# First attention of a four-layer kernel: one projection of queries and keys per batch, spread to head rows through DRAM

## The chip, the cores and the metric

The kernel runs on one NeuronCore of a Trainium2 chip. The metric is device time in microseconds (us) of the whole kernel, lower is better. The engines named are PE (TensorE, matmuls), DVE (VectorE), ACT (ScalarE), POOL (GpSimd) and SP (SyncE, which issues most of the DMAs). Each has its own queue of instructions, run in order, and they wait for each other by semaphores.

## The reference

Four layers, each an attention and a feed-forward part, over x of 4 batches x 512 tokens x 128 channels. The change touches the first attention only. It has H = 16 heads of 8 channels, a causal mask, and mixes the scores with a 3 x 3 kernel per head before the softmax:

```python
q = (x @ Wq).reshape(B, T, H, hd).transpose(0, 2, 1, 3)   # x normalised; k and v alike
attn = jnp.einsum('bhqd,bhkd->bhqk', q, k) * scale
kernels = softmax(kp.reshape(B, H, 9), axis=-1)           # kp from the context, per batch and head
attn0 = jnp.where(mask, 0.0, attn).reshape(1, B * H, T, T)
attn = conv(attn0, kernels 3x3, padding 1, one group per batch and head)
attn = jnp.where(mask, -jnp.inf, attn)
p = jax.nn.softmax(attn, axis=-1)
out = jnp.einsum('bhqk,bhkd->bhqd', p, v) ... @ proj_W + proj_b
```

## The kernel before, in words

A prologue (to about 82 us) loads weights, computes the 3 x 3 kernels from the context and builds constants. Then comes the first attention, `first_causal` (84 to about 465 us), with the start of the routing of the first feed-forward part. The rest isn't touched.

**The 3 x 3 mix as a matmul.** The score of a query row t and key column s after the mix is a sum over dy of queries shifted by dy and, over dx, of keys shifted by dx. So for each head 24 rows of the contraction are laid out: 3 shifts dy times 8 channels. `queries(G)` makes them for a group G of four heads (32 rows each, 128 in all) by three matmuls 128x512 against the weight tile `wq_rows`, which holds Wq's columns spread to these rows, each against a differently shifted x (`xnp`) and all added in one PSUM bank (bank 7). `keys(G)` is one matmul with `wk_rows`, which repeats a head's 8 columns three times. ACT copies the queries to `q3` (fp32) and, rounded, to `q3r`, and the keys to `kpad`. DVE mixes the keys over dx (`mixed_keys`: three instructions with a weight per row, `wcol`) into `kc`, ACT rounds that to `kcr`. Row 24 of each head carries the negated row maximum against a one in the keys.

**A group.** There are 16 groups G (four per batch b = G // 4). For each:
- far scores: 12 steps `max_scores` (L1379, fp32r matmuls of 32 rows into banks 0 and 1 in turn). DVE takes the maximum of each (`maxima`, L1694). Step n may start when the maximum of step n - 2 is taken.
- `maximum_out` puts the maxima in a tile, PE transposes it into bank 7 (`maximum_rows`, L1387), DVE adds it to `q3` (`maximum_in`, L1713).
- scores in three rounds (`scores`, L1400; the first needs `maximum_in`), exponentials on ACT (L1567), triangle select on POOL (L1296), product with v (`weighted`, L1411), copy, transposes, `outputs`.

**Near scores.** The entries next to the diagonal are computed apart, for one block of 128 tokens per group until group 10: `shifted` projections (L1365, three of them into bank 7, ACT copies L1552), products on POOL (`products`, L1282), sums on DVE (`near_scores`, L1675 to L1683).

**The order** is written out by hand for every engine. The loop over G interleaves: the far scores of group G + 1 (`top(0)` to `top(11)`), the three rounds of scores of group G, the queries and keys of group G + 2, the shifted projections and the weighted sums. On PE, after `maximum_rows`:

```python
top(0)
if G + 2 <= last:
    queries(G + 2)
top(1)
scores(G, 0)
top(2)
```

On DVE the iteration ends with `maximum_in(G + 1)` and then `near_scores(nb, nt)`; the next one begins with the maxima of the next group. Every use of bank 7 stands in a list (`plan`), and `take` waits until its last user has emptied the bank, so `queries` waits for `maximum_in`. At the end of a batch DVE also joins the four groups (`join`, L1735 to L1742) before `maximum_in`.

**Ahead of the attention.** POOL zeroes `wq_rows` and `wk_rows` (L327, L328) before its other constants, and DVE fills them by six copies (L537, L539). The last DMA that SP issues in the prologue fills `xs_d`, a DRAM buffer of 10.3 MB, with zeros (L291); nothing waits for it until the fourth batch is routed.

Of the kernel before, what the change touches and what calls it, by code (L numbers as in the profile page):

```python
# [10 lines left out]
ALU = mybir.AluOpType  # L11
ACT = mybir.ActivationFunctionType
F32 = mybir.dt.float32
# [7 lines left out]
P = 128  # L21
# [45 lines left out]
def build(nc, A, out, stop_after=99):  # L67
    with ExitStack() as ctx:
# [21 lines left out]
        row24 = sb("row24", [P, 1]); row8 = sb("row8", [P, 1])  # L90
# [50 lines left out]
        wq_rows = wide_rows[:, 0:12 * P].rearrange("p (a b c) -> p a b c", a=4, b=3)  # L141
# [66 lines left out]
        sel24 = arena[:, at[0] + NT * T // 4 + 2:at[0] + NT * T // 4 + 6]  # L208
# [24 lines left out]
        with nc.Block() as block:  # L233
            @block.sync
            def _(sp):
# [61 lines left out]
            def p_consts(ch):  # L297
# [8 lines left out]
                ch.link(nc.gpsimd.memset(sel24, 0.0))  # L306
                select(sel24, ALU.not_equal, 1.0, -24, [[-32, 4]], 1)
# [14 lines left out]
            def _(pool):  # L322
# [4 lines left out]
                nc.gpsimd.memset(wq_rows[:, :, :, :], 0.0)  # L327
                nc.gpsimd.memset(wk_rows[:, :, :], 0.0)  # L328
# [124 lines left out]
            def _(dve):  # L453
# [80 lines left out]
                dve.wait_ge(W["attn0"], wcount["attn0"])  # L534
                for dy in range(3):
                    src = lambda w: w.rearrange("p (g r d) -> p g r d", g=4, r=4)
                    nc.vector.tensor_copy(wq_rows[:, :, dy, :].rearrange("p g (r q) -> p g r q", r=4)[:, :, :, 8 * dy:8 * dy + 8],  # L537
                                          src(wq0))
                    nc.vector.tensor_copy(wk_rows[:, :, :].rearrange("p g (r q) -> p g r q", r=4)[:, :, :, 8 * dy:8 * dy + 8],  # L539
                                          src(wk0))  # L540

                dve.wait_ge(p_far, 1)
                ch.link(nc.vector.tensor_reduce(row24[:, :], sel24, AX_X, ALU.add))
# [12 lines left out]
            def _(act):  # L556
# [47 lines left out]
                            for v in (keep_all, mask_all))  # L604
# [15 lines left out]
        i0 = {n: lsem("i0_" + n) for n in ("qm", "s", "a", "c", "m", "p", "t", "pt", "o", "turn", "y")}  # L620

        c = {n: sem("c_" + n) for n in ("stats", "mean", "rstd", "xn", "nearw", "prod", "dots", "ne", "pb", "mm", "max", "mz", "kc",
                                        "kcr", "s", "exp", "sel", "pv", "pvout", "e", "ee", "num",
                                        "zero", "wide", "kv", "kT", "v", "kS", "kbd", "clean")}
        turn7 = sem("turn7"); free7_act = sem("free7_act"); free7_dve = sem("free7_dve")
# [545 lines left out]
        def first_causal():  # L1171
            at[0] = 0
            q3 = carve(3, T); kpad = carve(2, T + 2); kc = carve(3, T)
# [27 lines left out]
            plan("q", 1); plan("k", 1); plan("ln", 1)  # L1201
# [56 lines left out]
            with nc.Block() as block:  # L1258
                @block.gpsimd
# [72 lines left out]
                def _(pe):  # L1332
# [2019 lines left out]
```

## Time and profile before

| | |
|---|---|
| device time, median of 3 runs | 1663.72 us (1660.70 to 1664.81) |
| the profiled execution: its own time | 1674.48 us |
| the profiled execution: span | 1672.0 us |
| PE / DVE / ACT / POOL busy over the span | 1123.6 / 1042.1 / 524.1 / 587.0 us |
| mean granted TensorE clock | 0.784 |

The span runs from the first to the last instruction. The profiled execution is slower than the median of the unprofiled ones, so sums over the profile are held against its own time. Times are us, those of single instructions in the group view ns. A granted clock of 1.00 is 2.4 GHz, 0.50 is 1.2 GHz. One fp32 matmul is two instructions in the profile, and the profile merges repeats of a line into one row with their number (x6).

### The profile page before, as it was taken

Reading aid. Unit: us, or ns where it says so; the run is one execution under the profiler, and the core shown is the slowest. Engines: PE = TensorE matmul, PEld = TensorE weight load, DVE = VectorE, ACT = ScalarE, POOL = GpSimd, SP = SyncE. Lnnn points to the kernel's source line nnn. Section 1 sums busy time; section 2 is a strip of 40 time slices with the busy share of each in tenths; the row PEclk is TensorE's granted clock in tenths of the full one; section 3 lists DMA queues with packets and bytes.
Section 4 is the critical chain, followed back from the end, with each engine's and each line's share of the span. In section 5 each row is a group of like instructions: output and inputs, shape, how many; then the busy total and the mean of one; then the engine's idle time right before and its main releaser. Section 6 shows DMA issues by size and latency. Waiting matters only on the chain. (4 is left out here: it accounts for less than half of the span.)

```text
span 1672.0 us, 26006 instructions
## 1 busy us (share of the span) xinstructions
PE 1123.6 (67%) x9324; PEld 733.6 (44%) x9324; DVE 1042.1 (62%) x2995; ACT 524.1 (31%) x1045; POOL 587.0 (35%) x680
## 2 busy tenths in 40 slices
PE   1467988787868964556463399788648987856510
PEld 0333434343347963556463288433337943322200
DVE  2455676767643435999999466455434445668896
ACT  0123434443424532222221133144314513423300
POOL 7033323223341551101032544201345521256674
PEclk9978889998879985555555599888958997867665
DMA  4920000000032224444260112230002210022232
GB/s 118 314 69 1 1 1 1 1 1 13 11 101 70 71 77 113 101 113 113 64 153 14 42 58 61 67 110 1 17 27 63 72 59 13 11 79 81 83 102 73
DMA packets 74245, 106.19 MB, mean 64 GB/s; under 512 B 11501, under 2 KB 55712, under 8 KB 71616
## 3 DMA queue, kind: packets, MB, share of 16 engines
q1 hardware_dynamic: 59968, 72.16, 16.0%
q0 software_dynamic: 14144, 32.32, 6.4%
q8 instruction: 77, 1.26, 0.3%
q14 instruction: 56, 0.46, 0.1%
HBM read 77.10 MB, written 27.33 MB: 62 GB/s over the span
## 5 line engine op out<-in xcount | busy, mean ns | idle before, releaser
L856 POOL DMA_INDIRECT y_d<-arena,goal x138 | 132.6, 961 | 174.1 <-DVE arena L939 100.6
L1694 DVE CUSTOM_DVE_ANT_0 arena<-ps,far 128x512 f32<-128x512 f32 (+3 forms) x256 | 116.6, 488 | 64.3 <-PE ps L1379 62.6
L2033 POOL DMA_INDIRECT wide<-in_w_ud,arena x128 | 130.1, 1016 | 75.2 <-DVE arena L2064 38.8
L2953 PE MATMUL ps<-wide,arena 78*128 78x32 bf16 x3840 | 110.6, 187 | 47.7 <-ACT wide L3066 34.1
L2953 PEld LDWEIGHTS ps<-wide,arena 78*128 78x128 bf16 x3840 | 109.4, 104 | 54.3 <-ACT wide L3066 38.0
L1015 PEld LDWEIGHTS ps<-arena 128*128 128x128 f32 (+1 forms) x1012 | 123.3, 191 | 4.1
L1015 PE MATMUL ps<-arena 128*128 128x128 f32 (+1 forms) x1012 | 123.6, 274 | 0.0
L1296 POOL TENSOR_SCALAR_AFFINE_SELECT arena<-arena 128x520 f32<-128x520 f32 (+1 forms) x64 | 41.1, 654 | 154.9 <-ACT arena L1567 154.8
L1567 ACT ACTIVATE arena<-ps 128x1024 f32<-128x1024 f32 x80 | 78.4, 1022 | 50.9 <-PE ps L1400 50.6
L1379 PE MATMUL ps<-fr 32*128 32x256 f32 (+3 forms) x256 | 84.1, 409 | 14.1 <-DVE arena L1694 11.0
L1006 PE MATMUL ps<-arena 128*128 128x256 f32 x368 | 89.7, 387 | 1.6 <-DVE arena L915 1.6
L2577 DVE TENSOR_REDUCE arena<-ps 128x6 f32<-128x462 f32 (+1 forms) x96 | 55.2, 582 | 49.3 <-PE ps L2324 46.7
L1060 ACT ACTIVATE arena<-ps,arena 128x256 f32<-128x256 f32 x184 | 75.7, 471 | 30.1 <-PE ps L1006 30.0
L1379 PEld LDWEIGHTS ps<-fr 32*128 32x128 f32 x256 | 40.7, 192 | 87.2 <-DVE arena L1694 54.3
L939 DVE TENSOR_TENSOR arena<-ps,b_rows 128x256 f32<-128x256 f32 x46 | 19.6, 426 | 92.4 <-PE ps L1015 86.3
L2483 ACT ACTIVATE arena<-ps 77x1024 f32<-77x1024 f32 x64 | 65.1, 1020 | 38.3 <-PE ps L2341 36.9
L1352 PE MATMUL ps<-arena,wq_rows 128*128 128x512 f32 x96 | 64.9, 830 | 16.6 <-issue 15.8
L1282 POOL TENSOR_TENSOR arena<-arena 128x256 f32<-128x256 f32 (+2 forms) x48 | 47.7, 1020 | 76.1 <-ACT arena L1552 76.1
L1006 PEld LDWEIGHTS ps<-arena 128*128 128x128 f32 x368 | 67.8, 195 | 9.9 <-DVE arena L915 1.8
L2324 PE MATMUL ps<-fr 128*128 128x462 f32 (+1 forms) x96 | 50.5, 529 | 29.0 <-DVE arena L2577 23.7
L780 POOL DMA_INDIRECT xs_d<-arena,slot_i x48 | 47.6, 992 | 37.1 <-issue 24.7
L1400 PE MATMUL ps<-arena 32*128 32x256 f32 (+3 forms) x512 | 58.9, 482 | 2.3 <-DVE arena L1713 1.2
(514 smaller groups left out, 2570.2 us busy)
## 6 DMA issues: line engine op xcount, KB each, us to landing
arena<-low_d SPq DMA_DIRECT2D x32, 780.0 KB
xs_d<-zrow SPq DMA_DIRECT2D x1, 10320.0 KB, 39.8
arena<-xs_d SPq DMA_DIRECT2D x69, 129.0 KB, 2.1
arena<-y_d SPq DMA_DIRECT2D x16, 256.0 KB, 3.3
arena<-in_w SPq DMA_DIRECT2D x2, 1408.0 KB
y_d<-arena,goal POOLq DMA_INDIRECT x138
wide<-in_Wfc SPq DMA_DIRECT2D x1, 2048.0 KB, 11.9
wide<-in_Wproj SPq DMA_DIRECT2D x8, 256.0 KB, 6.7
```

Of the source, the lines that this page charges most:

```text
L856: pool.indirect_dma_start(out=y_d, in_=yb[:, i % 2, c, :], in_offset=None, out_offset=bass.IndirectOffsetOnAxis(ap=goal[:, i % 4, c:c + 1] ...
L1006: nc.tensor.matmul(ps[:, 1 + i % 2 * 2 + c // 2, c % 2 * BLK:c % 2 * BLK + BLK], w1s[:, i % 3, lo:lo + w], xT[:, i % 2, :], start=True, st ...
L1015: mm = nc.tensor.matmul(ps[:, 5 + i % 2, t * P:t * P + P], hT[0:w, i % 2, c, t * P:t * P + P], w2s[0:w, i % 3, c, :], start=c == 0, stop=c ...
L1060: nc.scalar.activation(hT[:, i % 2, c, :], ps[:, 1 + i % 2 * 2 + c // 2, c % 2 * BLK:c % 2 * BLK + BLK], act_fn, bias=b1s[:, i % 3, c:c + ...
L1352: mm = nc.tensor.matmul(bnk(7), wq_rows[:, G % 4, dy, :], xnp[:, G // 4 % 2, 1 + dy:1 + dy + T], start=dy == 0, stop=dy == 2)
L1379: mm = nc.tensor.matmul(ps[:, n % 2, 384 * i:384 * i + P * t + P], q3r[rows, G % 2, P * t:P * t + P], kcr[rows, G % 2, 0:P * t + P], start ...
L1400: mm = nc.tensor.matmul(ps[:, 2 + r, o:o + T - P * kt], kc[rows, G % 3, P * kt:P * kt + P], q3[rows, G % 3, P * kt:T], start=True, stop=True)
L1567: nc.scalar.activation(pt[:, r:r + heads, o:o + w], ps[:, 2 + r:2 + r + heads, 0:w], ACT.Exp, scale=SCALE)\
L1694: ins = nc.vector.tensor_tensor_reduce(junk[:, n % 2, 384 * i:384 * i + w], ps[:, n % 2, 384 * i:384 * i + w], far[:, T - w:T], 1.0, 3 * N ...
L2033: pool.indirect_dma_start(out=rows_g[t % 4][:, h, :], out_offset=None, in_=A["w_ud"], in_offset=bass.IndirectOffsetOnAxis(ap=eidi[:, t % 8 ...
L2483: nc.scalar.activation(pt[:, n % 3, :, :], ps[0:S2, 2 + rd * 2:4 + rd * 2, :], ACT.Exp, scale=SCALE)\
L2953: mm = nc.tensor.matmul(ps[:, 2 * (i % 3) + h // 2, col:col + 4 * HD], ring[m_ % 4][:, h * NK + p_, t % 2 * P:t % 2 * P + P], table[n // 4 ...
```

## The change: what it does

- Queries and keys are projected once per batch for all 16 heads, with Wq and Wk as they are (`queries(b)`, `keys(b)`: one matmul 128x512 each). ACT copies them to `qT0` and `kT_0`, two SBUF tiles that lie where `wq_rows` was.
- SP, which had nothing to do in this stage, stores them to two DRAM buffers (`spread(b)`): the queries three times, shifted by dy, into row dy of each channel, the keys three times by a broadcast. A channel has four rows there, the fourth is zero (filled in the prologue from `zrow`). Four rows of eight channels are a head's 32 rows.
- SP loads 128 rows of each for every group (`rows(G)`): queries to `q3`, keys to `kpad`, two groups ahead. It waits for the last reader of the buffer. The order of the rows changes from (dy, channel) to (channel, dy), so `wcol` and the row of the maximum (24, now 3) follow.
- ACT rounds `q3` to `q3r` from SBUF (`queries_rounded`) and has no copies of queries and keys per group any more.
- Per batch the projections stand at G = 3 and G = 7 (batches 2 and 3); those of batches 0 and 1 stand ahead of the loop, batch 1's now behind its normalisation.
- The first group's far scores start after two blocks of shifted projections instead of one, four steps for each block instead of three.
- `wq_rows`, `wk_rows`, their zeroing and the six copies go. Some semaphores are shared.

```diff
+        q_d = nc.dram_tensor("q_d", (2, P, 4, T), F32, kind="Internal").ap()
+        k_d = nc.dram_tensor("k_d", (2, P, 4, T), F32, kind="Internal").ap()
...
                 sp.wait_ge(p_const, 1)
+                for scratch in (q_d, k_d):
+                    wcount["misc"] += 16
+                    sp.dma_start(scratch[:, :, 3, :].rearrange("b h n -> h b n"), zrow[:, 0:T].unsqueeze(1).to_broadcast([P, 2, T]))\
+                        .then_inc(W["misc"], 16)
...
-                nc.gpsimd.memset(wq_rows[:, :, :, :], 0.0)
-                nc.gpsimd.memset(wk_rows[:, :, :], 0.0)
...
-                        dst = kk[:, gg * 3 + dx, :].rearrange("b (r q) -> b r q", r=4)[:, :, 0:24]
-                        last = nc.vector.tensor_copy(dst.rearrange("b r (y d) -> b r y d", y=3),
-                                                     kp4[:, gg, :, :, dx].unsqueeze(3).to_broadcast([B, 4, 3, HD]))
+                        dst = kk[:, gg * 3 + dx, :].rearrange("b (r d y) -> b r d y", r=4, y=4)[:, :, :, 0:3]
+                        last = nc.vector.tensor_copy(dst, kp4[:, gg, :, :, dx].unsqueeze(2).to_broadcast([B, 4, HD, 3]))
...
-                for dy in range(3):
-                    src = lambda w: w.rearrange("p (g r d) -> p g r d", g=4, r=4)
-                    nc.vector.tensor_copy(wq_rows[:, :, dy, :]...[:, :, :, 8 * dy:8 * dy + 8], src(wq0))
-                    nc.vector.tensor_copy(wk_rows[:, :, :]...[:, :, :, 8 * dy:8 * dy + 8], src(wk0))
...
-            plan("q", 1); plan("k", 1); plan("ln", 1)
+            plan("ln", 1); plan("q", 1); plan("k", 1)
...
-                if G + 2 <= last:
-                    plan("q", G + 2); plan("k", G + 2)
+                if G % 4 == 3 and G // 4 + 2 < B:
+                    plan("q", G // 4 + 2); plan("k", G // 4 + 2)
...
+                @block.sync
+                def _(sp):
+                    def spread(b):
+                        sp.wait_ge(free7_act, emptied(place7["q", b])[0])
+                        if b >= 2:
+                            for i in range(3):
+                                sp.wait_ge(landed_q[i], 16 * len(range(i, 4 * (b - 1), 3)))
+                        for dy in range(3):
+                            sp.dma_start(q_d[b % 2, :, dy, :], qT0[:, dy:dy + T]).then_inc(stored_q, 16)
+                        sp.wait_ge(free7_act, emptied(place7["k", b])[0])
+                        ...
+                        sp.dma_start(k_d[b % 2, :, 0:3, :], kT_0.unsqueeze(1).to_broadcast([P, 3, T])).then_inc(stored_k, 16)
+
+                    def rows(G):
+                        b, part = G // 4, slice(32 * (G % 4), 32 * (G % 4) + 32)
+                        sp.wait_ge(stored_q, 48 * (b + 1))
+                        sp.wait_ge(stored_k, 16 * (b + 1))
+                        if G >= 3:
+                            sp.wait_ge(c["s"], 3 * (G - 2))
+                        sp.dma_start(q3[:, G % 3, :], q_d[b % 2, part].rearrange("h y n -> (h y) n")).then_inc(landed_q[G % 3], 16)
+                        if G >= 2:
+                            sp.wait_ge(c["kc"], G - 1)
+                        sp.dma_start(kpad[:, G % 2, 1:T + 1], k_d[b % 2, part].rearrange("h y n -> (h y) n")).then_inc(landed_k[G % 2], 16)
+
+                    spread(0)
+                    rows(0)
+                    rows(1)
+                    spread(1)
+                    for G in range(G4):
+                        if G + 2 <= last:
+                            rows(G + 2)
+                        if G % 4 == 3 and G // 4 + 2 < B:
+                            spread(G // 4 + 2)
...
-                    def queries(G):
-                        take("q", G)
-                        pe.wait_ge(free7_act, emptied(place7["ln", G // 4])[0])
-                        for dy in range(3):
-                            mm = nc.tensor.matmul(bnk(7), wq_rows[:, G % 4, dy, :], xnp[:, G // 4 % 2, 1 + dy:1 + dy + T],
-                                                  start=dy == 0, stop=dy == 2)
-                        mm.then_inc(turn7, 1)
+                    def queries(b):
+                        take("q", b)
+                        pe.wait_ge(free7_act, emptied(place7["ln", b])[0])
+                        nc.tensor.matmul(bnk(7), wq0, xnp[:, b % 2, 2:2 + T], start=True, stop=True).then_inc(turn7, 1)
...
-                    def keys(G):
-                        take("k", G)
-                        nc.tensor.matmul(bnk(7), wk_rows[:, G % 4, :], xnp[:, G // 4 % 2, 2:2 + T], start=True, stop=True)\
-                            .then_inc(turn7, 1)
+                    def keys(b):
+                        take("k", b)
+                        nc.tensor.matmul(bnk(7), wk0, xnp[:, b % 2, 2:2 + T], start=True, stop=True).then_inc(turn7, 1)
...
                             if j == 0:
                                 pe.wait_ge(c["kcr"], G + 1)
+                                pe.wait_ge(c["q3r"], G + 1)
...
-                        max_scores(0, 3 * t, 3 * t + 3)
+                        if t:
+                            max_scores(0, 4 * t - 4, 4 * t)
+                    normed(1)
                     queries(1)
                     keys(1)
-                    normed(1)
...
-                        if G + 2 <= last:
-                            queries(G + 2)
+                        if G % 4 == 3 and G // 4 + 2 < B:
+                            queries(G // 4 + 2)
...
-                        nc.scalar.copy(q3[:, G % 3, :], bnk(7))
-                        nc.scalar.copy(q3r[:, G % 2, :], bnk(7)).then_inc(free7_act, 1)
+                    def queries_rounded(G):
+                        act.wait_ge(landed_q[G % 3], 16 * (G // 3 + 1))
+                        if G >= 2:
+                            act.wait_ge(c["mm"], 12 * (G - 1))
+                        nc.scalar.copy(q3r[:, G % 2, :], q3[:, G % 3, :]).then_inc(c["q3r"], 1)
...
                     def mixed_keys(G):
-                        dve.wait_ge(free7_act, emptied(place7["k", G])[0])
+                        dve.wait_ge(landed_k[G % 2], 16 * (G // 2 + 1))
```

## Rows read from the trace of the kernel before

**Rows 1.** Stretches: start:end length, busy per engine, clock, DMA share, GB/s.
```profile
core 0: us, PE busy (x) PEld busy (x) DVE busy (x) ACT busy (x) POOL busy (x), PEclk, DMA share, GB/s
140.00:465.00 325.00, 270.52 (x1675) 128.80 (x1675) 227.82 (x795) 138.68 (x234) 101.83 (x139) 0.90 0.01 4
```

**Rows 2.** Groups, 84 to 465 us, and one line's durations (ns, min/median/max).
```profile
L1352 PE MATMUL ps<-arena,wq_rows 128*128 128x512 f32 x96 | 64.9, 830 | 16.6 <-issue 15.8 <-ACT arena L1525 0.8
...
L1358 PE MATMUL ps<-arena,wk_rows x32: 592/697/1057, 97.4 to 426.3; 128*128 128x512 f32 x32
```

**Rows 3.** Timeline from 218.4 to 225.3 us: start, us, engine, line.
```profile
218.58 2.91 POOL L1282 TENSOR_TENSOR arena<-arena 128x256 f32<-128x256 f32 x3 [4.89 <-ACT arena L1552]
...
219.38 0.69 DVE L1713 TENSOR_TENSOR arena<-arena,ps 128x512 f32<-128x512 f32 x1 [0.81 <-PE ps L1387]
...
220.17 2.81 PE L1352 MATMUL ps<-arena,wq_rows 128*128 128x512 f32 x6 [0.41 <-issue]
...
221.53 1.35 DVE L1675 TENSOR_REDUCE arena<-arena 128x144 f32<-128x1152 f32 x1 [1.45 <-POOL arena L1282]
...
222.92 1.35 PE L1400 MATMUL ps<-arena 32*128 32x512 f32 x8
...
224.23 0.68 DVE L1694 CUSTOM_DVE_ANT_0 arena<-ps,far 128x512 f32<-128x512 f32 x1
...
224.98 0.50 PE L1379 MATMUL ps<-fr 32*128 32x384 f32 x2 [0.71 <-DVE arena L1694]
```

**Rows 4.** Timeline, PE and DVE rows of other turns (0, 5, 13, 14).
```profile
141.40 5.46 PE L1352 MATMUL ps<-arena,wq_rows 128*128 128x512 f32 x6 [5.48 <-issue]
...
247.43 0.66 DVE L1694 CUSTOM_DVE_ANT_0 arena<-ps,far 128x512 f32<-128x512 f32 x1
...
250.04 0.73 PE L1379 MATMUL ps<-fr 32*128 32x384 f32 x1
...
417.88 5.46 PE L1352 MATMUL ps<-arena,wq_rows 128*128 128x512 f32 x6 [0.18 <-issue]
...
436.54 0.69 DVE L1713 TENSOR_TENSOR arena<-arena,ps 128x512 f32<-128x512 f32 x1 [0.77 <-PE ps L1387]
...
449.66 0.68 DVE L1713 TENSOR_TENSOR arena<-arena,ps 128x512 f32<-128x512 f32 x1
```

**Rows 5.** Stretches as in rows 1, the seventh figure is the granted clock.
```profile
103.00:119.60 16.60, 14.59 (x32) 8.48 (x33) 11.92 (x33) 3.93 (x15) 6.95 (x7) 0.50 0.00 0
...
158.30:166.10 7.80, 5.17 (x21) 2.17 (x21) 5.36 (x18) 3.00 (x5) 3.51 (x4) 1.00 0.00 0
166.10:179.00 12.90, 12.90 (x84) 6.28 (x84) 8.79 (x35) 6.07 (x12) 4.59 (x12) 0.87 0.01 1
...
218.10:225.00 6.90, 5.17 (x21) 2.19 (x21) 4.46 (x11) 2.11 (x4) 3.51 (x4) 1.00 0.01 2
225.00:236.40 11.40, 11.38 (x84) 5.56 (x84) 8.77 (x35) 6.86 (x13) 1.87 (x3) 1.00 0.00 1
236.40:250.00 13.60, 7.06 (x17) 3.04 (x20) 11.28 (x25) 0.89 (x3) 4.40 (x4) 0.62 0.01 2
```

**Rows 6.** DMA issues: count, KB each, median us from issue to landing.
```profile
xs_d<-zrow SPq DMA_DIRECT2D x1, 10320.0 KB, 39.8
...
b_rows<-y_d SPq DMA_DIRECT2D x4, 256.0 KB, 3.0
```

**Rows 7.** Timeline of SP's last DMA and of the first group's keys.
```profile
55.10 0.63 SPq L291 DMA_DIRECT2D xs_d<-zrow  x1
...
99.23 0.55 DVE L1665 TENSOR_SCALAR arena<-arena,wcol,row 128x512 f32<-128x512 f32 x1 [8.37 <-ACT arena L1538]
...
102.06 0.50 PE L1379 MATMUL ps<-fr 32*128 32x512 f32 x2 [1.54 <-ACT fr L1544]
```

**Rows 8.** Timeline of the prologue.
```profile
1.56 1.38 POOL L327 MEMSET wq_rows<- 128x1536 f32 x1
2.87 0.53 POOL L328 MEMSET wk_rows<- 128x512 f32 x1
...
75.21 0.22 DVE L537 COPY wq_rows<-wqkv 128x128 f32<-128x128 f32 x1
```

More of the change, by code:

```diff
@@ L89, in build @@
         ident_bf = sb("ident_bf", [P, P], BF16)
[L90 removed]
+        row3 = sb("row3", [P, 1]); row8 = sb("row8", [P, 1])
         first_row = sb("first_row", [P, 1])
@@ L619, in build @@
         k = {n: sem("k_" + n) for n in ("stats", "mean", "rstd", "xn", "turn", "xnT", "sim", "seen", "idx", "dot", "act", "hv", "added")}
-        i0 = {n: lsem("i0_" + n) for n in ("qm", "s", "a", "c", "m", "p", "t", "pt", "o", "turn", "y")}
-        c = {n: sem("c_" + n) for n in ("stats", "mean", "rstd", "xn", "nearw", "prod", "dots", "ne", "pb", "mm", "max", "mz", "kc",
+        i0 = dict(zip(("qm", "s", "a", "c", "m", "p", "t", "pt", "o", "turn", "y"), k.values()))
+        loop_sems.extend(i0.values())
+        c = {n: sem("c_" + n) for n in ("stats", "mean", "rstd", "xn", "nearw", "prod", "dots", "ne", "pb", "mm", "max", "mz", "kc", "q3r",
                                         "kcr", "s", "exp", "sel", "pv", "pvout", "e", "ee", "num",
                                         "zero", "wide", "kv", "kT", "v", "kS", "kbd", "clean")}
+        landed_q = [sem(f"landed_q{i}") for i in range(3)]; landed_k = [sem(f"landed_k{i}") for i in range(2)]
+        stored_q = sem("stored_q"); stored_k = sem("stored_k")
         turn7 = sem("turn7"); free7_act = sem("free7_act"); free7_dve = sem("free7_dve")
@@ L1258, in first_causal @@
             with nc.Block() as block:
+                @block.sync
[8 more added lines that the diff above has]
+                        sp.wait_ge(free7_act, emptied(place7["k", b])[0])
+                        if b >= 2:
+                            for i in range(2):
+                                sp.wait_ge(landed_k[i], 16 * len(range(i, 4 * (b - 1), 2)))
+                        sp.dma_start(k_d[b % 2, :, 0:3, :], kT_0.unsqueeze(1).to_broadcast([P, 3, T])).then_inc(stored_k, 16)
[18 more added lines that the diff above has]
+                            spread(G // 4 + 2)
                 @block.gpsimd
@@ L1460, in _ @@
                         top(3)
-                        if G + 2 <= last:
-                            keys(G + 2)
+                        if G % 4 == 3 and G // 4 + 2 < B:
+                            keys(G // 4 + 2)
                         top(4)
@@ L1591, in _ @@
                             shifted(0, t, u)
-                        if t == 0:
+                        if t == 1:
+                            queries_rounded(0)
                             keys_rounded(0)
+                    normed(1)
                     queries(1)
                     keys(1)
-                    normed(1)
+                    queries_rounded(1)
                     keys_rounded(1)
@@ L1601, in _ @@
                         nb, nt = near_key(G)
+                        if G % 4 == 3 and G // 4 + 2 < B:
+                            queries(G // 4 + 2)
                         if G + 2 <= last:
-                            queries(G + 2)
+                            queries_rounded(G + 2)
                         exps(G, 0)
@@ L1606, in _ @@
                             outputs(G - 1)
-                        if G + 2 <= last:
-                            keys(G + 2)
+                        if G % 4 == 3 and G // 4 + 2 < B:
+                            keys(G // 4 + 2)
                         exps(G, 1)
@@ L1763, in _ @@
                     for t in range(NT):
-                        maxima(0, 3 * t, 3 * t + 3)
+                        if t:
+                            maxima(0, 4 * t - 4, 4 * t)
                         near_scores(0, t)
```

39 lines of the change are left out of this document (20 added, 19 removed).

## Prediction

> **What bounds the kernel now.** I read the view of stretches first, for the share of each engine in the first attention; then the groups of instructions there; then the timeline of one group of heads on all engines; then the stretches again, for TensorE's granted clock. In the main stretch PE is busy for 270.5 of 325 us and DVE for 227.8, at a mean clock of 0.90 [rows 1]. That reads as a stage bound by PE, of which the change takes a good part away: the 96 query matmul instructions (48 matmuls of two each) hold 64.9 us and the 32 key instructions about 0.70 us each, 22 us [rows 2]. After it 8 and 8 are left, each of some 0.47 us where the clock is full (2.81 us for six) [rows 3] and 0.9 us at half. So some 75 us of PE work go. The question is how many of them stand on the path.
>
> Call a turn what lies between one addition of the maxima (L1713) and the next; there are 16, numbered by G. Turn 4 is typical [rows 3]. L1713 begins at 219.38; the queries run 220.17 to 222.98, then one far score and the first round of scores to 224.27. The next PE instruction, the third far score at 224.98, waits for DVE (0.71 us idle, released by L1694). DVE takes its first maximum only at 224.23, because ahead of it in its queue stand the near scores (L1675, at 221.53), which waited for the products of POOL (218.58 to 221.49), which waited for the last shifted projection of the turn before. So the chain that sets the turn is: PE's block of work, shifted projection, ACT copy, POOL products 2.9, near scores 2.7, first maximum, PE's next block. The queries lie in the hole of that chain, and without them PE waits there longer: from about 221.5 instead of 224.3, still until 224.98. From there to 236.4 PE has no gap (11.38 of 11.40 us busy) [rows 5]; the keys are in that block.
>
> **The change part by part.** The sum is made against the profiled execution (1674.48 us, span 1672.0, which lies 10.8 us above the median 1663.72); I carry its difference over to the median.
>
> Start of the stage. Removed ahead of it: two POOL memsets, 1.38 + 0.53, and six DVE copies from 75.21 on, 0.8 together, so 2.7 us [rows 8]. Twelve small copies change only their pattern; two zero-fills of 512 KB each are issued on SP, which has nothing waited for early; I put both at nothing (cover gone: 1 MB, some 4 us). But the first queries now make a trip through DRAM: three stores of 256 KB and one of 768 KB, on the queue in which the 10.3 MB zero-fill stands, issued at 55.1 and landed 39.8 us later, at 94.9 [rows 6, 7]. The stores begin behind it, at the rate of that fill (10,320 KB in 39.8 us, 259 KB/us) take 5.9, end at 100.8; the load of a group (256 KB) lands in 3.0, the keys' issued behind it 0.5 later, 104.3; from the mixing of the keys to the first far score it is 102.06 - 99.23 = 2.8, so 107.1 against 102.06 now [rows 7]: 5 late. PE, POOL and DVE do two blocks of shifted projections meanwhile that they now do later, which returns most of it; but batch 1's queries and keys are now queued on PE behind its normalisation, a chain of norm, transposes, copy, projection, copy, projection, copy ahead of the next shifted projection, that adds about 3. I take +4.5, bounds 0 and +8. The gain of 2.7 in front is in it, as the zero-fill's end doesn't move with it.
>
> Turn 0. The queries are on the path: near scores are done before L1713, PE runs them at half clock, 5.46 us [rows 4], and the first scores wait behind them. -5.5, keys -0.6, together -6.1.
>
> Keys. A pair takes some 1.1 us at full clock (each at least 0.59, overlapping) [rows 2]. The sixth far score needs the fourth maximum, which DVE only begins when the fourth score is there; the keys cover that now. So I take half, 0.6 (bounds 0.3 and 1.1) in turns 1, 2, 4, 5, 6, 8, 9, 10: -4.8. Turns 3 and 7 still hold one projection each.
>
> Queries in turns 1 to 11: hidden in the hole, nothing, where the near scores bind. After a join of heads DVE is late with L1713 and PE runs the queries at half clock: in turn 5 DVE is ready at 247.43 + 0.6, the third score comes at 250.04 [rows 4]: -2.0, likewise turn 9: -4.0.
>
> Turns 12 and 13 have no near scores. Queries 2.8 and, at half clock, 5.46 [rows 4] are on the path, with the keys -3.4 and -6.1; turn 11 only keys, -0.6: -10.1. Turn 14 runs without any today: 436.54 to 449.66, 13.1 us, the shortest [rows 4].
>
> So far: 4.5 - 6.1 - 4.8 - 4.0 - 10.1 = -20.5.
>
> The DRAM trip in the turns. A group's load is issued once the last scores of the turn before are done (the last readers of its buffer), some 6 us ahead of where ACT has to have the queries rounded, before the first exponentials; it lands in 3.0 [rows 6]. ACT casts from SBUF (0.6) in place of two copies. Stores for batches 2 and 3 (turns 3, 7) have three turns until they are read. All nothing; behind a late load would stand ACT's exponentials, so every us late beyond a margin of about 3 would be a us of the turn.
>
> The clock. This is the term that decides. In turn 4 PE is busy 5.17 of the 6.9 us of the hole and keeps the full clock [rows 5]. 2.81 of these are queries. Without them some 2.4 of 6.9 are left, a third, with a dead stretch of 3.4 us at the end. What such stretches do the trace shows: after 236.4, where PE waits for a join, the clock is 0.62 over the stretch to 250; the opening, 103 to 119.6, stays at 0.50 for 16.6 us though PE is busy 14.6 of them, with small gaps [rows 5]. The price of a turn: in turn 1 the clock is at half in a part of the block (mean 0.87) and the block takes 12.9 against 11.4 us [rows 5], +1.5. If PE's small waits for DVE in the block, no longer covered by the keys, hold the half clock as in the opening, 9 us of the block run at half, +4.5. Between these I take 3.0, the middle: turns 2 to 10, nine, 27.0; turns 1 and 11, where it falls today too, 1.5 each; turns 0 and 13, whose half clock is today ended by the queries themselves, 2.5 each. +35. Bounds 0 (it never falls) and +54 (4.5 in eleven turns, 5 in the two).
>
> The Trainium skill (TensorE: Matmul & The Clock Gate, "HAM oscillation — how this bites in real kernels") says that bursts of matmuls parted by long enough waits each begin at half clock, so that the price is paid once in every iteration. That speaks against this change; by it all the turns fall, by the rows most do, since several stretches that are only two thirds busy keep the clock. The trace agrees with it at the joins. By its rule alone, at the price of turn 1, the sum would be near nothing.
>
> Sum: -20.5 + 35 = +14.5. The profile would show 1689; the median 1663.7 + 14.5 = 1678.2.
>
> **The rivals.** (a) The clock holds, and the kernel is faster. The mechanism: the score matmuls and far scores left in the hole, 2.4 us, are enough. For it: 158.3 to 166.1 has PE at 5.17 of 7.80 and a clock of 1.00 [rows 5]. Against: that is two thirds, not one third. Price: the 35 fall away, -20.5, 1643.2. It decides as soon as the mean loss of a turn is under 1.7 us (20.5 over 12). (b) The clock falls but costs only what it did in turn 1: 11 x 1.5 + 5, less 2, about 20: -0.5, 1663. For it: that is the one turn measured at full gap and half clock. (c) The clock stays low nearly through the block: +54 - 20.5 = +34, 1697. (d) The loads come late: 2 us over the margin in 14 turns is +28 on top of (b), 1691; against it, nothing else moves in the stage until POOL's scatters from turn 11 on. (e) The change takes nothing off because the stage is bound by DVE: not so where DVE is busy only 8.77 of the 11.4 us of the block [rows 5]; it would be -10, 1653.
>
> **How the numbers follow.** No change can be told from 0.3%, 5 us, either way. Chances: forecast 0.43, (a) 0.18, (b) 0.16, (c) 0.11, (d) 0.04, (e) 0.08. Slower: forecast, (c), (d) = 0.58; within 5 us: (b) = 0.16; faster: (a) and (e) = 0.26. The range runs from the foot of (a) to the top of (c): 1645 to 1700, leaving out about one in ten on either side. Both signs hold much, so the forecast's own range stands beside it: 1669 to 1690, clock terms of 2.2 to 4 us a turn.
>
> **What would show it.** The query and key groups at 8 instructions each, and the stage's PE busy share well under 0.83. The third far score in turns 1 to 10 still released by DVE's maximum, with an idle time near 3.5 us ahead of it where it is 0.7. The granted clock between the first and the last turn below 0.8, with blocks of 13 us and more (rival (a): at 0.95 and blocks near 11). The first L1379 some 5 us later. ACT's cast of the queries never waiting long for a DMA (rival (d): waits of microseconds there). I am wrong if the clock keeps full in the turns; and if the near scores, which I hold fixed, move forward with an earlier shifted projection by more than the block's gain.

## The result, and the profile after

The changed kernel takes 1698.53 us (median of 4 runs, 1692.86 to 1704.20) where the one before takes 1663.13 on the same chip: ratio 1.0215, 95% interval 1.0181 to 1.0250. It is slower by 35.4 us. The forecast was 14.5 slower; the time lies 1.5 us inside the top of the range, at rival (c) (1697). One execution of ten in each of two kernels below (tiny keys, and the last one) lies more than 1.5% above the fastest of its kernel; the ratios leave it out, the medians and ranges keep it.

The page of the profiled execution (own time 1695.52), its span, the busy times and the clock in 40 slices:

```profile
span 1693.0 us, 25810 instructions
...
PE 1110.5 (66%) x9212; PEld 733.7 (43%) x9212; DVE 1038.0 (61%) x2991; ACT 513.6 (30%) x1021; POOL 586.9 (35%) x678
...
PEclk8566877765578896555555579999977998876665
```

The first attention is slices 3 to 12. PE's busy time hardly fell (1123.6 before, 1110.5 now), though matmuls that had held some 75 us went: what is left runs at a lower clock. The groups (durations in ns, minimum/median/maximum) show that the change is in, 8 and 8 instructions in place of 96 and 32 [rows 2], and, of ACT's 16 casts of the queries (L1575), that one waited for a load, for 2.9 us:

```profile
L1385 PE MATMUL ps<-arena,wqkv x8: 592/1061/1192, 88.5 to 301.9; 128*128 128x512 f32 x8
...
L1389 PE MATMUL ps<-arena,wqkv x8: 1061/1142/1222, 91.2 to 312.5; 128*128 128x512 f32 x8
...
L1575 ACT CAST fr<-arena x16: 618/622/672, 101.7 to 443.8; 128x512 fp32r<-128x512 f32 x16
...
  DMA arena<-q_d: 2.9, 1
```

The same stretch as in [rows 1], then the 15 turns from the first addition of the maxima (L1755 now) to the last; columns as there, the clock is the seventh figure:

```profile
140.00:465.00 325.00, 242.35 (x1363) 120.34 (x1367) 211.76 (x712) 113.71 (x192) 91.32 (x124) 0.70 0.10 33
145.69:483.93 338.24, 256.33 (x1482) 128.32 (x1482) 220.80 (x765) 119.94 (x198) 90.75 (x126) 0.71 0.10 32
```

The same 15 turns of the kernel before:

```profile
140.62:449.66 309.04, 259.86 (x1587) 124.44 (x1587) 219.02 (x767) 131.36 (x223) 90.15 (x126) 0.91 0.01 3
```

The clock went from 0.91 to 0.71, PE's busy share from 0.84 to 0.76, and the last addition came 34.3 us later (483.93 against 449.66). That is nearly the whole difference of the medians (35.4). The code behind the last addition is the same in both; it takes 1209.1 us in this execution and 1222.3 in that of before, and between 1198 and 1225 in all fourteen profiles of this study, which is why the two spans differ by only 21.0. I therefore read the stage by its last addition, and the whole by the medians.

The turn that the prediction worked through, turn 4, in the timeline after, with PE and the two DVE rows that release it:

```profile
227.30 0.50 PE L1410 MATMUL ps<-fr 32*128 32x512 f32 x2
...
227.41 0.69 DVE L1755 TENSOR_TENSOR arena<-arena,ps 128x512 f32<-128x512 f32 x1 [0.82 <-PE ps L1418]
...
228.15 1.14 PE L1431 MATMUL ps<-arena 32*128 32x512 f32 x8 [0.35 <-DVE arena L1755]
...
229.56 1.35 DVE L1716 TENSOR_REDUCE arena<-arena 128x144 f32<-128x1152 f32 x1 [1.46 <-POOL arena L1316]
...
232.26 0.68 DVE L1735 CUSTOM_DVE_ANT_0 arena<-ps,far 128x512 f32<-128x512 f32 x1
...
233.01 0.76 PE L1410 MATMUL ps<-fr 32*128 32x384 f32 x2 [3.72 <-DVE arena L1735]
```

Beside [rows 3]: from the addition to DVE's first maximum it is 4.85 us in both kernels, and to PE's third far score 5.60 in both. PE merely waits 3.72 us there in place of 0.71. So the queries did lie in the hole and freed nothing. The hole and the block (whole, and cut in two), as stretches:

```profile
226.10:233.00 6.90, 2.22 (x15) 0.92 (x14) 4.45 (x11) 2.83 (x4) 4.15 (x5) 1.00 0.00 0
233.00:246.90 13.90, 12.97 (x82) 6.81 (x82) 8.98 (x35) 5.11 (x11) 1.23 (x2) 0.75 0.12 39
233.00:236.30 3.30, 2.45 (x13) 1.09 (x13) 2.15 (x11) 0.59 (x1) 0.00 (x0) 0.51 0.02 5
236.30:246.90 10.60, 10.52 (x69) 5.72 (x69) 6.83 (x25) 4.53 (x10) 1.23 (x2) 0.83 0.15 49
```

The hole itself still shows 1.00; the clock falls at its end, and the block begins at 1.2 GHz (0.51). In turn 4 it is back at 2.4 GHz about half-way, in turn 8 it doesn't come back within the block:

```profile
333.30:349.80 16.50, 16.08 (x69) 7.65 (x69) 7.68 (x29) 5.09 (x11) 1.23 (x2) 0.50 0.10 32
```

The third far score and the last shifted projection of turn 8, in the kernel after and in the kernel before:

```profile
329.97 0.79 PE L1410 MATMUL ps<-fr 32*128 32x384 f32 x2 [2.52 <-DVE arena L1735]
...
348.18 1.22 PE L1395 MATMUL ps<-wqkv,arena 128*128 128x256 f32 x2
```

```profile
312.65 0.49 PE L1379 MATMUL ps<-fr 32*128 32x384 f32 x2
...
323.38 0.70 PE L1365 MATMUL ps<-wqkv,arena 128*128 128x256 f32 x2
```

From the start of the one to the end of the other it is 19.4 us after and 11.4 before, where the keys were still among them.

The turns of the two kernels, from one addition to the next (us), worked out from the 16 rows of L1713 and L1755, and the granted clock of each:

| turn | 0 | 1 | 2 | 3 | 4 | 5 | 6 | 7 | 8 | 9 | 10 | 11 | 12 | 13 | 14 |
|---|---|---|---|---|---|---|---|---|---|---|---|---|---|---|---|
| before | 19.0 | 20.7 | 20.3 | 18.8 | 23.8 | 24.0 | 18.7 | 22.3 | 24.1 | 23.9 | 18.4 | 21.2 | 21.2 | 19.5 | 13.1 |
| after | 15.9 | 21.7 | 23.8 | 20.3 | 26.3 | 25.5 | 21.2 | 25.2 | 31.8 | 24.3 | 24.8 | 20.0 | 22.5 | 21.4 | 13.5 |
| clock before | 0.83 | 0.92 | 0.92 | 0.91 | 0.92 | 0.87 | 1.00 | 0.92 | 0.91 | 0.87 | 1.00 | 0.84 | 0.92 | 0.83 | 1.00 |
| clock after | 0.72 | 0.76 | 0.78 | 0.83 | 0.80 | 0.67 | 0.84 | 0.80 | 0.55 | 0.75 | 0.60 | 0.64 | 0.60 | 0.54 | 0.94 |

### The profile page after: what moved, and what is told of

It is laid out like the page before. It is cut to its first block and busy times, and to the rows that moved or that the text cites. A ratio compares the mean times of both kernels' runs of the same rounds, so it can differ in the third digit from the quotient of the medians.

```text
span 1693.0 us, 25810 instructions
## 1 busy us (share of the span) xinstructions
PE 1110.5 (66%) x9212; PEld 733.7 (43%) x9212; DVE 1038.0 (61%) x2991; ACT 513.6 (30%) x1021; POOL 586.9 (35%) x678
## 5 line engine op out<-in xcount | busy, mean ns | idle before, releaser
L1410 PE MATMUL ps<-fr 32*128 32x128 f32 (+3 forms) x256 | 94.6, 500 | 57.3 <-DVE arena L1735 51.6
L1410 PEld LDWEIGHTS ps<-fr 32*128 32x128 f32 x256 | 48.2, 245 | 133.3 <-DVE arena L1735 102.4
L1431 PE MATMUL ps<-arena 32*128 32x256 f32 (+3 forms) x512 | 79.1, 659 | 16.6 <-DVE arena L1755 15.2
L936 DVE TENSOR_TENSOR arena<-ps,b_rows 128x256 f32<-128x256 f32 x46 | 19.6, 425 | 94.8 <-PE ps L1012 94.8
L2369 PE MATMUL ps<-fr 128*128 128x462 f32 (+1 forms) x96 | 48.5, 508 | 30.9 <-DVE arena L2622 30.4
L1395 PE MATMUL ps<-wqkv,arena 128*128 128x384 f32 (+2 forms) x128 | 57.0, 573 | 3.9 <-ACT arena L1621 1.8
```

Of the source, the lines that this page charges most:

```text
L1395: mm = nc.tensor.matmul(ps[:, k7, o:o + w1_ - w0_], xnp[:, b % 2, col + off:col + off + P], wqkv0[:, w0_:w1_], start=True, stop=True)
L1410: mm = nc.tensor.matmul(ps[:, n % 2, 384 * i:384 * i + P * t + P], q3r[rows, G % 2, P * t:P * t + P], kcr[rows, G % 2, 0:P * t + P], start ...
L1431: mm = nc.tensor.matmul(ps[:, 2 + r, o:o + T - P * kt], kc[rows, G % 3, P * kt:P * kt + P], q3[rows, G % 3, P * kt:T], start=True, stop=True)
```

## The experiments

The theory: PE's queries cost nothing in the hole, and without queries and keys the clock drops. The rivals: the DRAM trip is what costs (late loads, or DMA traffic beside the matmuls), or the new order of the opening. All ratios below are to the kernel before on the same chip, with 95% intervals.

**1. The kernel before with less PE work, and no DRAM trip.** Both projections work on 8 of 512 columns, so the queries are nearly all stale values; all else is as before.

```diff
-   mm = nc.tensor.matmul(bnk(7), wq_rows[:, G % 4, dy, :], xnp[:, G // 4 % 2, 1 + dy:1 + dy + T],
+   mm = nc.tensor.matmul(ps[:, 7, 0:8], wq_rows[:, G % 4, dy, :], xnp[:, G // 4 % 2, 1 + dy:1 + dy + 8],
-   nc.tensor.matmul(bnk(7), wk_rows[:, G % 4, :], xnp[:, G // 4 % 2, 2:2 + T], start=True, stop=True)
+   nc.tensor.matmul(ps[:, 7, 0:8], wk_rows[:, G % 4, :], xnp[:, G // 4 % 2, 2:10], start=True, stop=True)
```

> The kernel before the change with the per-group query and key matmuls cut from 512 to 8 columns: the order, the waits and ACT's copies are those of before, only the PE work is gone, and there is no DRAM trip (the attention then computes with unfinished queries and keys). Clock theory: it is slower than before although it does less, 1680 to 1695, by the 28 us that the turns lost, without the 5 us of the opening. Rival (DRAM trip): it is faster than before by what the work was worth, 1640 to 1650.

Measured 1707.20 (1703.59 to 1708.89), 1.0287 [1.0243, 1.0331]. The kernel before is made 2.9% slower by taking work away from it, and nothing else, and by more than I expected (1680 to 1695). Its 15 turns, and its turn 2:

```profile
138.05:491.08 353.03, 298.90 (x1587) 162.06 (x1587) 221.09 (x766) 133.48 (x223) 90.35 (x126) 0.65 0.01 2
```

```profile
184.15:213.05 28.90, 26.27 (x109) 13.49 (x109) 14.32 (x48) 9.87 (x17) 7.21 (x10) 0.50 0.00 1
```

The last addition is 41.4 us later than before, at a clock of 0.65. PE does less and is busy 298.9 us in place of 259.9. In turn 2 it is busy 26.3 of 28.9 us: at half clock PE is the bound of a turn that takes 20.3 in the kernel before, at a clock of 0.92. DMA moves almost nothing here (a share of 0.01, 2 GB/s or less), so no DMA explains it. The output is wrong, as the queries are; behind the last addition the kernel takes 1213.5 us, within the range given above.

**2. Queries alone, and keys alone.** The same edit on one of the two projections.

> As the tiny projections, but only the queries are cut to 8 columns; the keys stay at 512 (queries unfinished). It splits the clock's loss: if the hole alone matters, it is as slow as the tiny projections or 5 us slower (1680 to 1700); if the keys, which cover PE's small waits inside the block, are what let the clock come back, it lies clearly under them, 1660 to 1675. Rival (DRAM trip): 1645 to 1655.

Measured 1684.26 (1674.39 to 1687.84), 1.0131 [1.0078, 1.0184], inside the wider of the two ranges expected (1680 to 1700).

> The kernel before, with only the key projection cut to 8 of its 512 columns (the mixed keys are then mostly stale values; the rest of the work is unchanged). With both projections cut the kernel was 2.9% slower than before, with the queries alone cut 1.3%. If each projection holds the clock for itself, the keys alone cost the difference: 1.5%, 1688. If the keys matter only once the queries are gone (the full hole brings the clock up, and the block keeps it), this kernel is within 0.4% of before or a few us faster (16 x 0.6 us of PE work gone): 1655 to 1668, with a granted clock above 0.88 from the first to the last addition.

Measured 1674.84 (1655.55 to 1696.80, 10 runs), 1.0057 [1.0023, 1.0092]. The keys alone cost 0.6%, the queries alone 1.3%, both 2.9%, more than their sum: neither of the two expectations for the keys alone came out. Of the 10.8 us by which the last addition comes later, 6.2 are in turn 5. PE's rows of that turn, first with the keys at 8 columns:

```profile
257.48 0.50 PE L1379 MATMUL ps<-fr 32*128 32x512 f32 x1
259.50 2.07 PE L1365 MATMUL ps<-wqkv,arena 128*128 128x384 f32 x4 [1.52 <-ACT arena L1584]
261.51 0.79 PE L1379 MATMUL ps<-fr 32*128 32x512 f32 x1
...
271.92 1.22 PE L1365 MATMUL ps<-wqkv,arena 128*128 128x256 f32 x2
```

and the same rows of the kernel before:

```profile
254.56 0.49 PE L1379 MATMUL ps<-fr 32*128 32x512 f32 x1
256.60 1.13 PE L1365 MATMUL ps<-wqkv,arena 128*128 128x384 f32 x4 [1.55 <-ACT arena L1584]
257.66 0.50 PE L1379 MATMUL ps<-fr 32*128 32x512 f32 x1
...
263.45 0.70 PE L1365 MATMUL ps<-wqkv,arena 128*128 128x256 f32 x2
```

Both wait 1.5 us for ACT at the same place. In one the clock falls there and stays at half to the end of the last projection shown, 13.6 us for what takes 7.6 in the other. Ahead of the wait the two differ by one key projection (0.39 in place of 1.12 us) and a gap of 0.24 us.

**3. The changed kernel with PE's work given back.** Three projections of full size, whose result nobody reads, in the hole: behind the first round of scores, to group 10; or in the old place ahead of it, to group 13 (groups 3 and 7 have the real projection there).

```diff
+   def fill(G, count):
+       for _ in range(count):
+           nc.tensor.matmul(bnk(7), wq0, xnp[:, G // 4 % 2, 2:2 + T], start=True, stop=True)
...
    scores(G, 0)
+   if G <= 10:
+       if G % 4 == 3:
+           pe.wait_ge(free7_act, emptied(place7["q", G // 4 + 2])[0])
+       fill(G, 3)
```

> The changed kernel with three extra matmuls 128x512 fp32 (2.8 us at full clock) into the free bank 7 right behind the first round of scores of groups 0 to 10, where PE waits for DVE's near scores; their result is not used. Clock theory: PE has more to do and the kernel gets faster, since the granted clock in the turns rises from about 0.7 to 0.9 or more: from 1698 to between 1655 and 1675. Rival (the DRAM trip, or a wait of the new order): the work is added for nothing, the time stays at 1698 or rises by up to 11 x 1 us where the filler runs past the hole.

Measured 1682.28 (1677.07 to 1691.08), 1.0156 [1.0106, 1.0207]; clock of the turns 0.83, last addition 19.1 us later than before. Nearly half of the loss is back, less than expected (1655 to 1675, at a clock of 0.9 or more).

```diff
    if G % 4 == 3 and G // 4 + 2 < B:
        queries(G // 4 + 2)
+   elif G + 2 <= last:
+       pe.wait_ge(free7_dve, emptied(place7["mz", G])[1])
+       fill(G, 3)
    top(1)
    scores(G, 0)
```

> The changed kernel with the three query matmuls' worth of PE work put back where the queries stood (ahead of the second far score, groups 0 to 13 but 3 and 7), result not used; the DRAM trip and the single projection stay. Clock theory: the turns come back to the length that they had before the change or 0.6 us less, the total to 1660 to 1672. Rival (DRAM trip or its waits cost the 35 us): stays within 5 us of 1698.

Measured 1667.63 (1655.74 to 1671.84, 9 runs), 1.0036 [1.0004, 1.0068]. Its turns:

```profile
147.09:459.62 312.53, 254.28 (x1555) 124.29 (x1555) 219.50 (x766) 118.45 (x198) 91.00 (x126) 0.88 0.10 35
```

Useless work makes the changed kernel 31 us faster (1698.53 to 1667.63), with every DMA of the change still there. With experiment 1 that settles it: nearly all of the loss is the clock, and not the DRAM trip. The last additions of the two fillings are 9.1 us apart; turn 5 alone makes 9.0 (31.8 against 22.8 us), and what the other turns differ by cancels. In turn 5 the 1.5 us wait for ACT again finds one of them at half clock behind it and the other not; ahead of it the filler stands behind the second far score and the first round of scores in the one, and ahead of them in the other.

**4. The keys' place too.** One more unread projection where the keys stood, beside the filling behind the scores, and (to group 13) beside the one in the old place.

```diff
    if G % 4 == 3 and G // 4 + 2 < B:
        keys(G // 4 + 2)
+   elif G <= 10:
+       fill(G, 1)
```

> The changed kernel with the filler of three matmuls in the hole and one more matmul 128x512 at the place that the keys of each group had (groups 0 to 10). If the small waits of PE inside the block, uncovered when the keys went, keep the half clock alive, it is faster than with the hole filled alone (1682): 1665 to 1675, with a clock of 0.86 or more in the stage. If the hole alone matters it is 1682 or up to 10 us more.

> The changed kernel, with projections whose result nobody reads in all the old places: three where the queries of a group stood, and now one where its keys stood. PE has about the work of before again, the rows still come from DRAM. Clock theory, whole: the kernel with the three alone was 0.36% over before; the keys' work holds the clock in the block, the stage comes to 309 to 312 us and the kernel to 1660 to 1668. Theory that the keys' place costs nothing by itself: the same as with three alone plus up to 0.6 us a turn, 1667 to 1676. Theory that the DRAM trip costs something besides the clock: over 1675.

Measured 1685.50 (1682.07 to 1693.52), 1.0121 [1.0088, 1.0154], and 1672.21 (1668.16 to 1683.06), 1.0094 [1.0058, 1.0131]. The first can't be told from its fellow without the fourth projection, the second is if anything slower than its own (the intervals just touch). So with the hole filled a projection in the keys' place brought nothing that can be measured, against the 1665 to 1675 and 1660 to 1668 that I expected if it did. Why cutting the keys alone cost 0.6% in experiment 2, with the queries whole, is not explained by that.

**5. The opening.** First the 10.3 MB zero-fill is issued behind the first loads, so that no store of queries can wait for it.

```diff
-   sp.dma_start(xs_d.rearrange("(p a b) d -> p a (b d)", p=P, b=4), zrow[...]...)   # prologue
...
    spread(1)
+   sp.dma_start(xs_d.rearrange("(p a b) d -> p a (b d)", p=P, b=4), zrow[...]...)
    for G in range(G4):
```

> The changed kernel with the 10.3 MB zero-fill issued by SP behind the stores of batch 1 instead of at the end of the prologue. If the opening's 5 us are the wait of the first stores behind that fill, the first group's keys land some 3 to 4 us earlier and the first addition of the maxima (145.7 us in the changed kernel) begins at 141 to 143; total down by 2 to 5 us, unless the clock takes it back. Rival (the trip itself, stores plus loads, or batch 1's projections queued behind its normalisation): first addition stays at 145 or later.

Measured 1729.92 (1723.08 to 1734.00), 1.0380 [1.0348, 1.0411]. The first mixing of keys comes at 100.76 in place of 101.67, and the first addition not earlier at all (146.15 against 145.69). So it wasn't the fill. The whole was expected 2 to 5 us faster or unchanged and came out some 25 us slower than the changed kernel. It cost, instead, what rival (d) describes: SP's queue of DMA issues (start, duration) shows the load of group 2 stuck behind the fill,

```profile
132.84 0.64 SPq L1285 DMA_DIRECT2D xs_d<-zrow  x1
133.58 23.83 SPq L1276 DMA_DIRECT2D arena<-q_d  x1
157.45 0.61 SPq L1279 DMA_DIRECT2D arena<-k_d  x1
```

and turn 0 takes 36.1 us in place of 15.9. In the changed kernel itself PE, ACT and POOL have this at the end of the opening:

```profile
124.58 1.15 PE L1379 MATMUL ps<-ident,arena 128*128 128x128 f32 x4 [3.30 <-DVE arena L1696]
...
126.51 2.05 PE L1385 MATMUL ps<-arena,wqkv 128*128 128x512 f32 x2 [0.77 <-ACT arena L1557]
...
129.23 2.08 PE L1389 MATMUL ps<-arena,wqkv 128*128 128x512 f32 x2 [0.68 <-ACT wq_rows L1563]
...
131.98 2.08 PE L1395 MATMUL ps<-wqkv,arena 128*128 128x384 f32 x4 [0.68 <-ACT wq_rows L1569]
...
138.85 2.91 POOL L1316 TENSOR_TENSOR arena<-arena 128x256 f32<-128x256 f32 x3 [14.29 <-ACT arena L1589]
```

Batch 1's projections (L1385, L1389) stand at half clock between its normalisation and the next shifted projections (L1395), for which POOL waits 14.29 us. So they were moved into turn 0, where those of batches 2 and 3 stand in turns 3 and 7:

```diff
-   plan("ln", 1); plan("q", 1); plan("k", 1)
+   plan("ln", 1)
...
-   if G % 4 == 3 and G // 4 + 2 < B:
-       queries(G // 4 + 2)
+   if G in (0, 3, 7):
+       queries((G + 5) // 4)
```

The keys, the list of uses of bank 7 and the stores change alike.

> The changed kernel, with batch 1's projections of queries and keys moved out of the opening into the places of turn 0 that those of batches 2 and 3 have in turns 3 and 7. If the 5 us that the opening became longer come from these two projections, which stand on PE and ACT behind batch 1's normalisation and ahead of the next shifted projections at half clock, the first addition comes at 141 to 143 in place of 145.7. If they come from the DRAM trip, it stays at 145 to 146. Turn 0 gets about 1 us longer. The whole: 1693 to 1698, as the clock in turns 1 to 13 stays low.

Measured 1692.05 (1689.06 to 1695.55), 1.0199 [1.0162, 1.0236]. The first addition is back where it was before:

```profile
140.92 0.69 DVE L1750 TENSOR_TENSOR arena<-arena,ps 128x512 f32<-128x512 f32 x1 [0.23 <-issue]
```

The 4.8 us of the opening are these two projections. The turns stay slow (clock 0.70): turn 4 took 31.6 us here and 26.3 in the changed kernel. The ratio can't be told from the changed kernel's 1.0215.

**6. Two ideas for the kernel before.** The scores ahead of the queries on PE (and the exponentials ahead of the queries' copies on ACT), and six unread projections in the joins of heads.

```diff
    top(0)
-   if G + 2 <= last:
-       queries(G + 2)
    top(1)
    scores(G, 0)
+   if G + 2 <= last:
+       queries(G + 2)
```

> The kernel before the change with the queries of group G + 2 put behind the first round of scores of group G (on PE, and on ACT behind its exponentials): the same work, but in the hole where PE waits for DVE. Clock theory: the hole is as full as before, the scores no longer wait behind the queries where they bind (turns 0, 5, 9, 12, 13), so 3 to 12 us faster than before. Rival (the order of the queries doesn't matter, or ACT's later copies of them bind): within 3 us of before.

```diff
+   if G % 4 == 0 and G >= 4:
+       pe.wait_ge(c["max"], 12 * (G + 2) - 1)
+       for _ in range(6):
+           nc.tensor.matmul(bnk(0), wk_rows[:, 0, :], xnp[:, G // 4 % 2, 2:2 + T], start=True, stop=True)
    if G + 1 <= last:
        maximum_rows(G + 1)
```

> The kernel before the change with six idle-time matmuls 128x512 (result not used) in front of the transposes of the maxima at the three joins of heads (groups 4, 8, 12), where PE waits some 6 us for DVE and the clock falls. Clock theory: the queries behind each join run at full clock, 2.8 us instead of 5.4, so 2 to 3 us less for each: 5 to 9 us faster than before. Rival (the time there is set by DVE alone): no change, within 3 us.

Measured 1668.35, 1.0012 [0.9985, 1.0039], and 1674.30, 1.0017 [0.9992, 1.0043], 12 runs each: neither can be told from no change, where 3 to 12 and 5 to 9 us faster were expected. The filled joins make turns 9 and 13 shorter (22.4 and 16.6 us against 23.9 and 19.5) and turn 5 longer (30.4 against 24.0).

**7. The changed kernel, mended.** The filler in the old place from turn 1 on, and batch 1's projections in turn 0.

```diff
+   elif G and G + 2 <= last:
+       pe.wait_ge(free7_dve, emptied(place7["mz", G])[1])
+       fill(G, 3)
...
-   if G % 4 == 3 and G // 4 + 2 < B:
+   if G in (0, 3, 7):
```

> The changed kernel with both mendings: three unread projections in the old place of the queries from turn 1 on (none in turn 0, where nothing covers them), and batch 1's projections in turn 0. By the clock theory the turns 1 to 13 are those of the kernel with the filler in all turns (1667.6, 0.36% over before), turn 0 is 4 to 6 us shorter and the opening 3 to 4: 1658 to 1662, a little faster than before. If turn 0's filler is what brought the clock up for turn 1, turn 1 is 2 us longer, 1660 to 1664. If the clock falls back in the later turns, 1675 or more.

Measured 1660.58 (1647.97 to 1674.36, 10 runs), 1.0010 [0.9981, 1.0039], inside the expected 1658 to 1662, and not to be told from before. Its turns:

```profile
138.86:448.52 309.66, 252.66 (x1553) 124.38 (x1553) 219.56 (x766) 120.12 (x201) 89.96 (x126) 0.88 0.12 40
```

All the profiles together say the same thing. For each kernel, how much later than before its last addition came in the profile, the clock of its turns, and the distance of the medians (us):

| kernel | last addition | clock | median |
|---|---|---|---|
| changed, zero-fill ahead of a load | +55.2 | 0.69 | +60.6 |
| before, both projections tiny | +41.4 | 0.65 | +44.9 |
| changed | +34.3 | 0.71 | +35.4 |
| changed, batch 1 in turn 0 | +32.4 | 0.70 | +30.3 |
| before, tiny queries | +23.6 | 0.75 | +22.0 |
| changed, hole filled | +19.1 | 0.83 | +20.0 |
| changed, hole and keys' place filled | +19.6 | 0.83 | +16.2 |
| before, tiny keys | +10.8 | 0.88 | +13.1 |
| changed, both old places filled | +9.3 | 0.89 | +10.5 |
| changed, old place filled | +10.0 | 0.88 | +5.3 |
| before, joins filled | +4.9 | 0.92 | +5.0 |
| before, scores first | +3.3 | 0.90 | -1.0 |
| changed, filled and batch 1 moved | -1.1 | 0.88 | -1.2 |

The kernel before has 0.91. The clock and the delay run together to within a few us, but for the zero-fill, whose delay is in good part the late load; the filled joins, 4.9 us late at the highest clock of all, with work added; and the last row, which starts 1.8 us ahead and has a shorter turn 0. The profile is one execution of each kernel, the median is of 4 to 12.

## Why the prediction was right in direction and too small

The direction, the mechanism and the place were right; one term was mis-sized, the clock's: 35 forecast, and 54.2 worked out from the turns. Set out by turns, with the prediction's removals and clock price netted, and the measured difference from the table of turns:

| part | forecast | measured |
|---|---|---|
| opening | +4.5 | +5.1 |
| turn 0 | -6.1 + 2.5 = -3.6 | -3.1 |
| turn 1 | -0.6 + 1.5 = +0.9 | +1.0 |
| turns 2, 3, 4, 6, 7 | 5 x 3.0 - 3 x 0.6 = +13.2 | +12.9 |
| turns 5, 9 | 2 x (3.0 - 2.6) = +0.8 | +1.9 |
| turns 8, 10 | 2 x (3.0 - 0.6) = +4.8 | +14.1 |
| turn 11 | -0.6 + 1.5 = +0.9 | -1.2 |
| turn 12 | -3.4 | +1.3 |
| turn 13 | -6.1 + 2.5 = -3.6 | +1.9 |
| turn 14 | 0 | +0.4 |
| sum | +14.5 | +34.3 |

- **Removals.** Right where they can be read apart: the hole has the same length in both kernels, the third far score is still released by DVE (3.72 us idle, 3.5 forecast), and turn 0 gives back what the queries held there.
- **The clock's price.** 3.0 us a turn was right in turns 2 to 7 and 9, where it came to 3.1 on average. In turns 8, 10, 12 and 13 it was wrong by 19.5 of the 19.8 us that are missing. With the removals taken as forecast, the clock costs 54.2 us in all (29.2 for the turns, and 25.0 of removals), at the top bound of +54 and not at the 35 chosen. The step that failed is the price of a turn: I took 9 us at half clock as the worst case (4.5 us) and the middle under it (3.0), while a turn in which the clock doesn't come back within the block costs 7.0 (turn 10) and 8.3 (turn 8, 19.4 us for the work of 11.4). The prediction's own row of the opening, 16.6 us at 0.50 with PE busy for 14.59 [rows 5], had shown a clock that stays at half for longer than 9 us. Turn 12 I gave no price at all, without a reason, though its queries went as well, and it costs 4.7; turn 13 I gave 2.5, and it is 8.0. In turn 11 the clock fell too (0.64) and cost nothing: PE is busy there for only 13.7 of 20.0 us.
- **The rule.** The Trainium skill (TensorE: Matmul & The Clock Gate, "HAM oscillation — how this bites in real kernels") has each burst behind a long wait begin at half clock. The trace agrees in turn 4, where the block begins at 0.51 and is at full clock half-way. Turn 8 begins so too, but PE is then busy for 16.08 of 16.50 us with the clock at 0.50 to the end: what I had drawn from the rule, that the price is small and paid once in an iteration, doesn't hold there.
- **The opening.** The sum was right (+5.1), its parts less so. The first far score comes at 104.49, 2.4 us late and not 5: the first loads were issued at 98.0 and not at 100.8, and without the zero-fill ahead of the stores (experiment 5) the keys' mixing began only 0.9 us earlier. The larger part is batch 1's projections at half clock on the path of the near scores, which I had at 3 and which experiment 5 puts at 4.8.
- **The rivals.** (a) and (b) fell, as the clock fell in every turn and cost twice the 1.5 us of turn 1 in turns 2 to 7 and 9. The range was said to start at the foot of (a), but (a) stood at 1643, under its 1645. (d) fell: the loads landed in 2.6 and 3.0 us, ACT's casts waited 2.9 us in all, DVE's mixing of keys only in the opening (13.2 us, where it had waited 8.4 for ACT before), and the fillers gave the time back with all loads in place. Its mechanism exists (turn 0 with the zero-fill ahead of a load), but not in this kernel. (e) fell as DVE's work in the turns hardly differs (219.0 and 220.8 us) while they became 29.2 us longer. (c) is what happened, in four turns (8, 10, 12, 13) rather than in all, so that its sum (+34) comes so near by luck.

What stays open is what decides, block by block, whether the clock comes back. Turn 5 took 30 us or more in five of the fourteen profiles and under 26 in nine, and I have no rule for it from these runs. Why the filler behind the scores lets turn 5 fall and the one ahead of them doesn't is seen in one profile of each, not explained.

## What to carry to other kernels

Work that hides in a wait of TensorE can be what keeps the engine at full clock for the work behind the wait. Before such work is taken out, look at the granted clock in the stretch around the wait, and price the next block at half clock, to its end and not only at its start, as the upper bound. The cheap test is the one that settled it here: cut the suspected matmuls to a few columns in the kernel as it is, and see whether it gets slower; then take the work out only where PE is on the path (turn 0 here, 17.0 us in the last kernel against 19.0), and leave the rest. Here that came out even with the kernel before, no better.

## What the runs showed of the hardware that I had not expected

- Less work on TensorE made a kernel 2.9% slower with no other edit (1662 to 1707 us), and unread matmuls made one 1.8% faster (1698.53 to 1667.63).
- TensorE busy for 16.08 of 16.50 us stayed at 1.2 GHz throughout (turn 8 after), and 13.64 of 13.70 us in turn 5 with tiny keys, while other blocks at half clock came back to 2.4 GHz half-way.
- Behind a wait of 1.5 us the clock was lost for 13.6 us of matmuls in one kernel and kept in another, whose work ahead of the wait differed by under 1 us (one profile of each).
- SP's issue of a 256 KB load stood for 23.83 us behind a fill of 10.3 MB that SP had issued just before it (132.84 and 133.58 us).
